# Half of the attention's score blocks mirrored on TensorE, with masks moved behind the exponential

## What is computed

```python
h = relu(layernorm(x))
norm2 = norm(h, axis=1, keepdims=True)
cos = beta * (h @ h.T) / (norm2 @ norm2.T + 1e-07)
P = softmax(cos + (1.0 - adj) * -1e9, axis=1)
x = x + P @ h
h = relu(layernorm(x))
deg = clip(sum(adj, axis=1, keepdims=True), 1.0)
x = x + h @ W_self + (adj @ h / deg) @ W_neigh
```

## Time and profile before

| | us |
|---|---|
| three runs: lowest, median, highest | 531.8, 533.44, 533.96 |
| the profiled execution | 531.57 |
| its span, first to last instruction | 529.8 |
| TensorE busy | 491.7 |
| VectorE busy | 405.3 |
| ScalarE busy | 340.3 |
| GpSimd busy | 338.4 |

### The profile page before, as it was taken

How to read it: one execution, slowest core, us unless ns; L and a number is a source line. 1 busy time by engine, 2 the same in 40 slices (tenths; PEclk the granted TensorE clock), 3 DMA queues, 4 the chain that set the end, 5 groups by cost and what they waited for, 6 DMA issues and landing times.

```text
span 529.8 us, 12739 instructions
## 1 busy us (share of the span) xinstructions
PE 491.7 (93%) x5280; PEld 378.5 (71%) x5280; DVE 405.3 (76%) x700; ACT 340.3 (64%) x357; POOL 338.4 (64%) x382
## 2 busy tenths in 40 slices
PE   0178999999999999999999999999979999999996
PEld 0146777777777777777777777777768988889895
DVE  6989877999999999999999999999955123231253
ACT  2959876888798888788788878889971111101111
POOL 3889999877997997998898899798751000000000
PEclk9979999999999999999999999999998999999998
DMA  8034457555575666657556557566300000000001
GB/s 251 26 113 166 161 161 230 172 197 157 174 234 171 222 185 215 186 182 231 170 189 208 191 172 236 177 216 193 97 4 1 21 21 1 21 21 21 22 1 41
DMA packets 43710, 72.29 MB, mean 136 GB/s; under 512 B 2432, under 2 KB 10880, under 8 KB 43648
## 3 DMA queue, kind: packets, MB, share of 16 engines
q1 hardware_dynamic: 43648, 71.44, 43.2%
HBM read 69.34 MB, written 2.10 MB: 135 GB/s over the span
## 4 chain that ended last, share of the span: by engine, by line
PE 80%; POOL 8%; DVE 6%; issue 4%; DMA 1%; ACT 0%; SPq 0%; DVEq 0%; POOLq 0%
PE ps L933 21%; PE ps L860 10%; PE ps L875 9%; PE ps L862 9%; PE ps L843 9%; PE ps L845 9%; PE ps L844 9%; POOL adjm L355 2%; POOL adj_t L357 2%; PE ps L920 2%; PE ps L909 2%; DVE adj_t L548 1%; DVE adj_t L579 1%; DMA x_sb<-in_x_dram 1%; POOL table L310 1%
## 5 line engine op out<-in xcount | busy, mean ns | idle before, releaser
L497 ACT ACTIVATE e_hi<-ps,small 128x1024 f16<-128x1024 f32 x128 | 154.1, 1204 | 57.1 <-DVE ps L707 55.5
L707 DVE SCALAR_TENSOR_TENSOR ps<-adjm,small,ps 128x1024 f32<-128x1024 fp8e4 x128 | 164.2, 1283 | 16.7 <-POOL adjm L355 13.3
L715 DVE TENSOR_TENSOR e_lo<-ps,e_hi 128x1024 f16<-128x1024 f32 x128 | 156.0, 1218 | 2.1 <-ACT ps L498 1.5
L498 ACT ACTIVATE ps<-ps,small 128x1024 f32<-128x1024 f32 x128 | 149.7, 1169 | 0.0
L355 POOL TENSOR_SCALAR adjm<-stage 128x1024 uint8<-128x1024 f32 x128 | 133.7, 1045 | 17.0 <-DMA stage<-in_adj_dram 6.6
L357 POOL TENSOR_SCALAR adj_t<-stage 128x1024 uint8<-128x1024 f32 x128 | 133.8, 1045 | 10.2
L860 PE MATMUL ps<-table,e_hi 128*128 128x129 f16 x1024 | 131.8, 221 | 0.4
L862 PE MATMUL ps<-table,e_hi 128*128 128x128 f16 x1024 | 131.6, 218 | 0.0
L933 PE MATMUL ps<-table,adj_t 128*128 128x257 f16 x1024 | 118.7, 276 | 2.8 <-POOL table L379 2.8
L933 PEld LDWEIGHTS ps<-table,adj_t 128*128 128x128 fp8e4 x1024 | 99.9, 99 | 17.1 <-POOL table L379 3.1
L860 PEld LDWEIGHTS ps<-table,e_hi 128*128 128x128 f16 x1024 | 99.0, 97 | 18.2 <-issue 2.8
(11 more groups left out here) (90 smaller groups left out, 273.0 us busy)
## 6 DMA issues: line engine op xcount, KB each, us to landing
stage<-in_adj_dram SPq DMA_DIRECT2D x128, 512.0 KB, 4.3
x_sb<-in_x_dram SPq DMA_DIRECT2D x4, 512.0 KB, 6.2
out_dram<-x_sb SPq DMA_DIRECT2D x7, 256.0 KB, 2.3
out_dram<-x_sb SPq DMA_DIRECT2D x1, 192.0 KB, 2.1
stage<-in_L_gnn_W_neigh_dram SPq DMA_DIRECT2D x1, 64.0 KB, 1.8
stage<-in_L_gnn_W_self_dram SPq DMA_DIRECT2D x1, 64.0 KB, 1.9
out_dram<-x_sb SPq DMA_DIRECT2D x1, 64.0 KB, 1.5
small<-in_L_gnn_beta_dram SPq DMA_DIRECT2D x1, 0.5 KB, 2.8
```

The lines of the kernel that those rows point to most:

```text
L497: act.activation(ring(e_hi, n), scored(n), ACT.Exp, bias=exp_bias, scale=exp_scale).then_inc(s_ehi, 1)
L498: act.activation(scored(n), scored(n), ACT.Exp, bias=exp_bias, scale=exp_scale).then_inc(s_exp, 1)
L707: dve.scalar_tensor_tensor(scored(n), ring(adjm1, n), mask_scale, scored(n), ALU.mult, ALU.add).then_inc(s_masked, 1)
L715: dve.tensor_tensor(ring(e_lo, n), scored(n), ring(e_hi, n), ALU.subtract).then_inc(s_elo, 1)
```

## The change

The order of the work comes from `pair_order`: in step s only the pairs at and right of the diagonal are computed, 72 instead of 128. 56 of these, the ones off the diagonal, also serve their mirror image. k counts the pairs and m those with a mirror.

- No mask ahead of the exponential. ScalarE reads the scores of one 512-column chunk as soon as its three products are done and writes the float16 high part into the upper half of each 32-bit word of `word`; VectorE writes the rest into the lower half. The step of both halves is two 16-bit elements.
- VectorE multiplies the words, seen as float32, by adj as 0 or 1: the near mask, `word` times `adj_t`, both in SBUF, into `near`.
- For a pair with a mirror TensorE transposes the eight 128 x 128 blocks of words in float32 into two PSUM banks (`TURN` and the next), each transpose behind a score product of the pair after it. VectorE multiplies them by the other adjacency tile into `far`. There is one such set of banks: `turn` waits for the far mask ahead of it (`s_far`) and for the words (`s_elo`); the far mask waits for all eight (`s_turn`).
- Both, near and far, go to TensorE as strided float16 weights, 24 products each. Near rows gather in PSUM as before; far rows go to one bank (`far_acc`), and VectorE adds them to `x_sb` after every mirrored pair (`spill`). So `x_sb` holds sums with the denominator (130 columns a tile) and x is loaded a second time, 256 KB per step.
- GpSimd converts each adjacency tile once (128 in all), straight into `adj_t`, three pairs ahead, with two slots for near tiles and two for far ones; the array is packed on the host so that each tile is 512 KB in one piece. The first two conversions stand between the small powers of the first layer norm.
- Score banks hold one chunk each, three of them, instead of three pairs of banks.
- At a step's start `evacuate` moves the accumulators of the step ahead, `new_rows` divides, adds x and the mean of h for rows with no edge; statistics follow one pair later, scales two. ScalarE and GpSimd make that step's part of the second table during the attention for steps 0 to 4, and behind it for 5 to 7. ScalarE also makes all high halves of the first table.
- The mean's 64 products become four of VectorE's partial sums and four products. In the aggregation the first group's last four row blocks come behind the first eight of the second group.

The diff, cut to its core (the lines that go stand in the code printed above):

```diff
--- before.py
+++ after.py
...
+    PAIR, _, _ = pair_order(N)
+    NP = len(PAIR)
+    FAR = [k for k in range(NP) if PAIR[k][2]]
+    NT = len(FAR)
+    FAR_BEFORE = [sum(m < k for m in FAR) for k in range(NP + 1)]
+    FIRST = [min(k for k in range(NP) if PAIR[k][0] == s) for s in range(NS)] + [NP]
...
+        stage = sb("stage", [P, 4 * TILE], fp32)
+        word = sb("word", [P, 2 * TILE], fp32)
+        near = sb("near", [P, 2 * TILE], fp32)
+        far = sb("far", [P, 2 * TILE], fp32)
+        x_again = sb("x_again", [P, ROWS], fp32)
...
+        def score(k, c):
+            return ps[:, 5 + (2 * k + c) % 3, :]
+        def turned(k, c):
+            return ps[:, TURN + c, :]
...
+        def half(buffer16, k, c, t, part, tiles=1):
+            at = 2 * (k % 2 * TILE + c * ROWS + t * P) + part
+            return buffer16[:, at:at + 2 * tiles * P].rearrange("p (n two) -> p n two", two=2)[:, :, 0] if part == 0 else \
+                buffer16[:, at - 1:at - 1 + 2 * tiles * P].rearrange("p (n two) -> p n two", two=2)[:, :, 1]
...
+            for k in range(NP):
+                s = PAIR[k][0]
+                if k >= 2:
+                    sp.wait_ge(s_adjd, k - 1)
+                sp.dma_start(stage[:, k % 2 * TILE:(k % 2 + 1) * TILE], adj_in[tile]).then_inc(s_near_in[k % 2], 16)
+                tile += 1
+                if PAIR[k][2]:
+                    m = FAR_BEFORE[k]
+                    if m >= 2:
+                        sp.wait_ge(s_adjt, m - 1)
+                    sp.dma_start(stage[:, (2 + m % 2) * TILE:(3 + m % 2) * TILE], adj_in[tile]).then_inc(s_far_in[m % 2], 16)
+                    tile += 1
+                for again in range(NS):
+                    if k == min(FIRST[again] + 8, NP - 1):
+                        load_x_again(again)
...
+            def convert(k):
+                slot = k % 2
+                pool.wait_ge(s_near_in[slot], (k // 2 + 1) * 16)
+                pool.tensor_scalar(adj_tb[:, near_adj(k)], stage[:, slot * TILE:(slot + 1) * TILE], FP8_ONE, 0.0,
+                                   ALU.mult, ALU.add).then_inc(s_adjd, 1)
+            def convert_far(k):
+                m = FAR_BEFORE[k]
+                slot = 2 + m % 2
+                pool.wait_ge(s_far_in[m % 2], (m // 2 + 1) * 16)
+                if k == FIRST[2]:
+                    pool.wait_ge(s_tab, NS)
+                    pool.wait_ge(s_mean, 1)
+                pool.tensor_scalar(far_adj(k, adj_tb), stage[:, slot * TILE:(slot + 1) * TILE].rearrange("p (t c) -> p t c", t=TPS),
+                                   FP8_ONE, 0.0, ALU.mult, ALU.add).then_inc(s_adjt, 1)
             inverse_std(0)
+            convert(0)
             inverse_std(1)
+            convert(1)
...
+            for k in range(NP):
+                s, at = PAIR[k][0], k - FIRST[PAIR[k][0]]
+                if k + LEAD < NP:
+                    convert(k + LEAD)
+                    if PAIR[k + LEAD][2]:
+                        convert_far(k + LEAD)
+                if s == 0 and k % 2 == 0 and k // 2 + 1 < NS:
+                    low_parts(k // 2 + 1)
+                if 1 <= s <= 6 and at == 4 - s // 6:
                     scales_of_x2(s - 1)
...
+            def exps(k, general):
+                if k >= 2:
+                    act.wait_ge(s_near, k - 1)
+                    if PAIR[k - 2][2]:
+                        act.wait_ge(s_turn, FAR_BEFORE[k - 1])
+                if general:
+                    load_inverse_norms(k)
+                for c in range(2):
+                    if general:
+                        act.wait_ge(s_scaled, 2 * k + c + 1)
+                    act.wait_ge(s_scores, 2 * k + c + 1)
+                    act.activation(half(word16, k, c, 0, HIGH, TPS), score(k, c), ACT.Exp, bias=exp_bias, scale=exp_scale)
+                    act.activation(score(k, c), score(k, c), ACT.Exp, bias=exp_bias, scale=exp_scale).then_inc(s_exp, 1)
...
+                for k in range(NP):
+                    s, at = PAIR[k][0], k - FIRST[PAIR[k][0]]
+                    exps(k, general)
+                    if s == 0 and k < 4:
+                        table_high(4 + k)
+                    if 1 <= s <= 5 and at == 6 - s // 5:
+                        second_h(s - 1)
+                        second_high(s - 1)
 
...
                     dve.tensor_scalar(mean_h[:, :], ps[:, 0, 3 * D:4 * D], 1.0 / (HS * N), None, ALU.mult
                                       ).then_inc(s_mean, 1)
+                for b in range(2):
+                    rows = x_v3[:, s * TPS + 2 * b:s * TPS + 2 * b + 2, 0:D + 1]
+                    if s == 0:
...
+            def new_rows(s):
+                dve.wait_ge(s_evac, 2 * (s + 1))
+                then(dve.tensor_scalar(den_s, x_v3[:, s * TPS:(s + 1) * TPS, D], HS, 1e-30, ALU.mult, ALU.max))
                 then(dve.reciprocal(rden, den_s))
+                dve.tensor_scalar(ne_p, den_s, 1e-30, 1.0, ALU.is_le, ALU.mult)
+                dve.wait_ge(s_xr, 16 * (s + 1))
...
+            def low_part(k, c):
+                dve.wait_ge(s_exp, 2 * k + c + 1)
+                dve.tensor_tensor(half(word16, k, c, 0, LOW, TPS), score(k, c), half(word16, k, c, 0, HIGH, TPS), ALU.subtract
+                                  ).then_inc(s_elo, 1)
...
+            def mask_near(k):
+                dve.wait_ge(s_adjd, k + 1)
+                dve.wait_ge(s_elo, 2 * (k + 1))
+                if k >= 2:
+                    dve.wait_ge(s_pvd, k - 1)
+                dve.tensor_tensor(ring(near, k), ring(word, k), adj_t[:, near_adj(k)], ALU.mult).then_inc(s_near, 1)
+            def mask_far(k):
+                m = FAR_BEFORE[k]
+                dve.wait_ge(s_turn, m + 1)
+                dve.wait_ge(s_adjt, m + 1)
+                if m >= 2:
+                    dve.wait_ge(s_pvt, m - 1)
+                dve.tensor_tensor(
+                    ring(far, m).rearrange("p (c t n) -> p c t n", c=2, t=TPS),
+                    ps[:, TURN:TURN + 2, :].rearrange("p c (t n) -> p c t n", t=TPS),
+                    far_adj(k, adj_t).rearrange("p t (c n) -> p c t n", c=2), ALU.mult).then_inc(s_far, 1)
+            def spill(k):
+                s, p, _ = PAIR[k]
+                rows = x_v3[:, 2 * p:2 * p + 2, 0:D + 1]
+                dve.wait_ge(s_pvt, FAR_BEFORE[k] + 1)
+                if s == 0:
+                    dve.tensor_copy(rows, two_rows(FAR_ACC)).then_inc(s_spill, 1)
+                else:
+                    if k == FIRST[s]:
+                        dve.wait_ge(s_spill, FAR_BEFORE[k])
+                    dve.tensor_tensor(rows, two_rows(FAR_ACC), rows, ALU.add).then_inc(s_spill, 1)
...
+                for k in range(NP):
+                    s, at = PAIR[k][0], k - FIRST[PAIR[k][0]]
+                    if s >= 1 and at == 0:
                         evacuate(s - 1)
+                    if k + 1 < NP and PAIR[k + 1][2]:
+                        mask_far(k + 1)
+                    if k + 1 < NP:
+                        mask_near(k + 1)
+                    if k + 2 < NP:
+                        words(k + 2, general)
+                    if PAIR[k][2]:
+                        spill(k)
+                    if s == 0 and 3 <= k < 3 + TPS:
+                        partial_sum(k - 3)
+                    if s >= 1 and at == 0:
...
+            def score_product(k, c, i):
+                s, p, _ = PAIR[k]
+                q = 2 * k + c
+                if i == 0 and q >= 3:
+                    pe.wait_ge(s_elo, q - 2)
+                j = unit_lo(2 * p + c, 1) if i == 0 else unit_hi(2 * p + c, 1)
+                rows = unit_lo(s * TPS, TPS) if i == 1 else unit_hi(s * TPS, TPS)
+                ins = pe.matmul(score(k, c), j, rows, start=i == 0, stop=i == 2)
+                if i == 2:
+                    ins.then_inc(s_scores, 1)
+            def turn(k, c, t):
+                m = FAR_BEFORE[k]
+                if c == 0 and t == 0 and m >= 1:
+                    pe.wait_ge(s_far, m)
+                if t == 0:
+                    pe.wait_ge(s_elo, 2 * k + c + 1)
+                ins = pe.transpose(turned(k, c)[:, t * P:(t + 1) * P], ring(word, k, c, 1)[:, t * P:(t + 1) * P], ident)
+                if c == 1 and t == TPS - 1:
+                    ins.then_inc(s_turn, 1)
...
+            def scores_and_turns(k, n):
+                new, flip = k < NP, n < NP and PAIR[n][2]
+                for i in range(8):
+                    if new and i < 6:
+                        score_product(k, i // 3, i % 3)
+                    if flip:
+                        turn(n, i // TPS, i % TPS)
+            def attend_far(k):
+                s, p, _ = PAIR[k]
+                m = FAR_BEFORE[k]
+                pe.wait_ge(s_far, m + 1)
+                if m >= 1:
+                    pe.wait_ge(s_spill, m)
                 for c in range(2):
                     for t in range(TPS):
+                        rows = s * TPS + t
```

(47 more changed lines are left out.)

611 lines of the change are left out of this document (267 added, 344 removed).

## The result

The changed kernel takes 560.04 us (median of four, 558.26 to 563.32); the kernel before, run beside it, 533.08. The ratio is 1.052, with a 95% interval from 1.049 to 1.056: 5.2% slower, where 1.9% was forecast. The profiled execution has a span of 558.7 us, where the prediction had 540.1.

The account below looks back on a forecast made before the run. TensorE was taken to stay the bound by busy time; first product 46.5, its work 314.7, chain 13.9 + 11.9, port 9.3 and rows 6 end the attention at 402.3, span 540.1, forecast 543.8 us, 1.9% slower; range 512 to 580.

Parts of the forecast that it names:

- TensorE's sum: TensorE's work in the attention: 4.91 us per mirrored pair, 2.66 per plain one, 318.6 in all.
- the ring: Mirrored pairs in succession: last transpose, far mask, near mask, first word half, next first transpose; 5.24 us per round.
- The rival of a cheap chain: Mirrored pairs: transpose loads hide and no mask waits for GpSimd, so faster, 517 us; chance 0.28.
- The chain: Handovers between TensorE and VectorE for mirrored pairs: 5.24 us against 4.91 of work; 13.9 + 11.9 us over 49 successions.
- The near mask against GpSimd: VectorE's near mask, two SBUF operands, waits for running conversions: 0.19 us on average, 9.3 us on 49 successions.
- rival 2: Every near mask waits out a GpSimd conversion, 0.8 us instead of 0.19: 30 us more, 574; chance 0.11.
- The strided weights: Attention products read every second 16-bit value as weights; the slower load was taken at nothing, with 160 us as bound.
- Rival 3: Strided weight loads of the attention products don't hide: 584 us at a quarter of the bound, about 700 at all; chance 0.12.
- The transposes: Eight float32 transposes per mirrored pair on TensorE, 0.11 us apart, 0.88 together; the skill page's 275 ns each was rejected.
- fit into the slack: Statistics and partial sums of h on VectorE cost nothing within the 1.4 us that the chain leaves it.
- The start: Before the attention: GpSimd's powers delayed, 1 us to the first transposes; first attention product at about 46.5 us, not 43.07.
- Rows renewed: Some eleven small VectorE operations at a step's end overrun the slack by 1.0 us, six times: 6 us.

Follow-up runs that it names:

- the ninth run: Changed kernel with ScalarE's new rows of step 4 moved behind pair 67's exponentials and GpSimd's half behind its last conversion; 559.55 us, ratio 1.052.

## Why the prediction was right or wrong, point by point

**The bound and the sign: right.** TensorE's sum of 4.91 for a mirrored pair and 2.66 for a plain one held, as the runs with the ring taken away show (4.91 to 4.93, 2.70). The rival of a cheap chain was to decide under 5.2; the period was 5.32. The prediction's sign for being wrong, a clock that falls in mirrored steps, showed in one place only, the first 4.4 us of the attention.

**The chain: right, each link within 0.05.** 5.32 where 5.24 was worked out: the word half took 0.72 and not 0.67 (it writes every second value; side by side it was 0.68), and the handover 0.15, not 0.12. On 49 successions that is 0.08 each, 4 us. Counting the pair order again gives 50 successions behind a mirrored pair and 6 behind a plain one, where the text had 42 and 7: 8 x 0.33 - 1.70 = 0.9 us more.

**The near mask against GpSimd: right in kind, the size in part by luck.** Forecast 9.3 us, measured 9.1 over the 22 held masks; but the 9.3 were for the mirrored pairs, on which only 6.9 lie. The row of all 72 in the changed kernel:

```profile
L767 DVE TENSOR_TENSOR near<-word,adj_t x72: 1206/1216/2081, 47.4 to 416.6; 128x1024 f32<-128x1024 f32 x72
```

Minimum, median and maximum are 1.21, 1.22 and 2.08, as "minimum near 1.24, maximum near 2.2" had it. The 29 gaps of mirrored pairs among mirrored ones are 0.50 over TensorE's work on average; the sum had 0.33 + 0.19 = 0.52. Most masks are untouched, so rival 2 is out. The longest of them, with the conversion that was running when it began:

```profile
67.09 1.05 POOL L380 TENSOR_SCALAR adj_t<-stage 128x1024 uint8<-128x1024 f32 x1
67.13 2.08 DVE L767 TENSOR_TENSOR near<-word,adj_t 128x1024 f32<-128x1024 f32 x1
```

It ends at 69.21, 1.07 behind the conversion's end, so nearly its whole usual length lies behind it. The rule quoted from the Trainium skill, "SBUF — State Buffer", on the shared port pair, stands. It reaches further than the prediction took it: the row work has two inputs in SBUF too, and the sum had no term for that. In the changed kernel the row work of the steps 1 to 6 happened to meet no conversion; in several of the later runs it did.

**The strided weights: right to leave them at nothing.** The weight loads of lines 976 to 979 take 97 to 99 ns (median), as before, and the products go 0.057 apart or less. Rival 3 is out.

**The transposes: right.** At full clock three start 0.11 apart (0.49 for three in the timeline above); the 275 ns of the Trainium skill's "TensorE: Matmul & The Clock Gate", Part 4, which it gives for a bfloat16 block, lies by the recorded length of one here (0.27), not by the pace. So "the trace disagrees" compared a length with a pace.

**The step that failed: the terms around the steady state.** The span lies 18.6 us over the sum, 4 of it by the chain's links. What failed are the terms that the prediction put at nothing ("fit into the slack"), at an average, or at a wrong place in the order:

- The last four plain pairs, 7.0 us. Their gaps are 5.40, 3.47, 3.13 and 3.05, together 15.05, where TensorE's work is 2.66 + 2.66 + 1.37 + 1.37 = 8.06. That the statistics fit into the slack was worked out for mirrored pairs, where VectorE has 1.4; in a plain pair it has some 0.3. VectorE's timeline there has no idle time from 401.52 to 417.7, and spreading the row work gained nothing at these four (14.9):

```profile
401.52 1.21 DVE L767 TENSOR_TENSOR near<-word,adj_t 128x1024 f32<-128x1024 f32 x1
402.66 1.34 DVE L750 TENSOR_TENSOR word<-ps,word 128x512 f16<-128x512 f32 x2
...
404.70 1.13 DVE L706 SCALAR_TENSOR_TENSOR x_sb<-x_sb,small,x_again 128x128 f32<-128x128 f32 x4
405.87 1.14 DVE L712 SCALAR_TENSOR_TENSOR x_sb<-mean_h,small,x_sb 128x128 f32<-128x128 f32 x4
406.92 1.22 DVE L767 TENSOR_TENSOR near<-word,adj_t 128x1024 f32<-128x1024 f32 x1
```

- Pairs 3 to 11, 3.7 us: 8.4 over TensorE's work, where 9 x 0.52 = 4.7 were in the sum. The run with GpSimd held back has the same order and shows the parts: 3.1 us less there, the collisions, for which 9 x 0.19 = 1.7 stood in the sum. Averaged over the stage GpSimd is busy 0.37, but in step 0 its tiles come one behind another. And in that run the pairs 5 to 8 still stand at 5.70 and not 5.32: the four partial sums of h, of 1.96 us each, don't fit into the 1.4, another 1.5 us that the prediction had at nothing.
- The start, 2.8 us: first product at 49.28, not 46.5. VectorE's unit rows (line 631, otherwise 0.28, so 0.7 for three) fell on two conversions and a table part of GpSimd's, 2.2 us; the first near mask took 1.71, another 0.5. This is read from the trace, no run tests it:

```profile
30.65 2.96 DVE L631 TENSOR_SCALAR adj_t<-adj_t 128x128 f32<-128x128 f32 x3
...
30.38 1.05 POOL L380 TENSOR_SCALAR adj_t<-stage 128x1024 uint8<-128x1024 f32 x1
31.39 1.05 POOL L392 TENSOR_SCALAR adj_t<-stage 128x1024 uint8<-128x1024 f32 x1
32.40 1.13 POOL L355 TENSOR_TENSOR table<-adj_t,table 128x512 f16<-128x512 f32 x1
```

  The transposes wait for these rows. The rows of the kernel before had shown just this, up to 1.06 us, and the sum used it for the mask only.
- Pair 66, 1.4 us: the jam that the ninth run took away, 8.16 where 4.91 + 1.89 = 6.80 was expected. ScalarE's new rows wait for GpSimd and VectorE, and what is queued behind them, the exponentials of pair 66, wasn't looked at.
- The tail, 1.6 us: 139.4 from the last product, not 137.8. The text had 144 products before the last table is needed, and counted on step 7's. Step 6's is needed after 96, and GpSimd has it late:

```profile
419.24 10.79 PE L1040 MATMUL ps<-table,adj_t 128*128 128x257 f16 x96
431.89 13.02 PE L1040 MATMUL ps<-table,adj_t 128*128 128x257 f16 x116 [1.86 <-POOL table L428]
```

  Of the 3.0 us lost at this place in the earlier trace rows, 1.86 are still there. The 3.3 us at the lower clock are gone in the profiled execution.

These are 16.5 us and the chain's 4, together 1.9 us more than the miss. Of these 1.0 is the row work in step 6, counted in the six at 1.0 as well as in the last plain pairs, and 0.7 the chain's links in the pairs 3 to 11, counted twice as well; the rest, of both signs, is spread over the pairs at the ends of the steps and wasn't taken apart. Rows renewed came near the forecast: 1.2 over the period at the third pair of four steps, 2.0 in step 5.

So the one large term was sized well, and the forecast still had only 10 of the 27 us of the loss: what lies outside the steady state was taken at its average or at nothing, and it lies where the averages don't hold (at the start, in the first step, in the short last steps).
